# Three-column products and reordered outer products in the stencil stage of a convolution, attention and expert kernel

## The reference, cut to what matters

```python
offset = x1 @ off_w + off_b
mask = jax.nn.softmax((x1 @ mask_w + mask_b).reshape(N, H, W, G, P), -1)
...
samples = _bilinear_sample(img, sg)
out = (samples * m).sum(-1)
return out @ out_w + out_b
```

## Time and profile before

| what | value |
|---|---|
| median of three runs | 676.95 us |
| the profiled execution, its own time | 677.6 us |
| span of its trace | 675.7 us |
| busy: PE / DVE / ACT / POOL | 600.9 / 555.7 / 234.7 / 318.5 us |
| mean granted TensorE clock | 0.97 |
| products L1656 | 208 instructions, 216.8 us busy |
| outer products L1588, additions L1597 | 55.5 and 45.0 us busy |

### The profile page before, as it was taken

One profiled execution on the slowest core, in us unless ns is written; L12 is line 12 of the kernel. 1 busy time (PEld: TensorE's weight loads), 2 busy tenths in 40 slices (PEclk: granted clock), 3 DMA queues, 4 the chain that ended last, 5 costly groups with the idle time before them and its releaser, 6 DMA issues.

```text
span 675.7 us, 11172 instructions
## 1 busy us (share of the span) xinstructions
PE 600.9 (89%) x3668; PEld 448.7 (66%) x3668; DVE 555.7 (82%) x1028; ACT 234.7 (35%) x351; POOL 318.5 (47%) x408
## 2 busy tenths in 40 slices
PE   5989968979889889889696789999999999989995
PEld 4557556657567667666474677777777777785774
DVE  4677999999999999999999889847677766654877
ACT  6172504405207116135034000254544544415431
POOL 7504876787578588658578500202222211115222
PEclk9899989989999899899998899999999999989999
DMA  6196402103003007000000000000000000004111
GB/s 182 44 352 206 138 0 81 34 2 110 1 4 110 1 3 275 0 1 3 0 2 4 0 1 1 1 1 0 1 1 1 1 1 1 0 2 125 42 39 47
DMA packets 26244, 30.76 MB, mean 46 GB/s; under 512 B 5573, under 2 KB 18325, under 8 KB 26197
## 3 DMA queue, kind: packets, MB, share of 16 engines
q1 hardware_dynamic: 24094, 29.77, 13.4%
q0 software_dynamic: 1408, 0.36, 0.7%
q10 hardware_dynamic: 694, 0.01, 0.1%
HBM read 25.07 MB, written 5.05 MB: 45 GB/s over the span
## 4 chain that ended last, share of the span: by engine, by line
PE 44%; DVE 33%; issue 11%; ACT 2%; DVEq 0%; DMA 0%; SPq 0%; POOL 0%; ACTq 0%; POOLq 0%
DVE prod L1656 18%; PE banks L1061 9%; PE pair L1041 8%; PE banks L934 8%; DVE outer L1588 6%; PE pair L1129 4%; PE banks L1051 4%; PE banks L1167 4%; DVE hats L1539 1%; PE banks L921 1%; DVE stencil L1597 1%; PE banks L1012 1%; PE pair L864 1%; PE banks L956 1%; PE banks L1033 1%
## 5 line engine op out<-in xcount | busy, mean ns | idle before, releaser
L934 PE MATMUL banks<-ident,prod 128*128 128x128 f32 x1440 | 209.0, 288 | 44.6 <-DVE prod L1656 43.2
L934 PEld LDWEIGHTS banks<-ident,prod 128*128 128x128 f32 x1440 | 170.1, 147 | 99.4 <-DVE prod L1656 74.5
L1656 DVE TENSOR_TENSOR prod<-shifted,stencil 128x1024 f32<-128x1024 f32 (+1 forms) x208 | 216.8, 1084 | 7.6 <-ACT stencil L599 4.2
L1412 POOL TENSOR_TENSOR rstd_now<-mv_now,neg_half 128x2 f32<-128x2 f32 x32 | 23.0, 719 | 134.1 <-DVE mv_now L1704 134.1
L864 PE MATMUL pair<-xg,dw_diag 128*128 128x512 f32 x144 | 72.5, 604 | 1.4 <-DVE xg L1466 1.4
L1307 POOL DMA_INDIRECT got<-padded,cell_now x44 | 62.6, 1423 | 19.0 <-issue 10.1
L1061 PEld LDWEIGHTS banks<-shifted 128*128 128x128 f32 x512 | 60.2, 192 | 8.1 <-issue 6.1
L1061 PE MATMUL banks<-shifted 128*128 128x128 f32 x512 | 63.3, 277 | 2.3 <-ACT shifted L740 1.4
L1041 PE MATMUL pair<-shifted 128*128 128x512 f32 x128 | 60.6, 596 | 0.1
L1719 DVE TENSOR_REDUCE neg_max<-pair 128x1 f32<-128x1024 f32 x32 | 39.2, 1225 | 23.1 <-PE pair L1041 21.9
L1588 DVE TENSOR_TENSOR outer<-hats 128x800 f32<-128x800 f32 x56 | 55.5, 990 | 1.8 <-PE banks L921 1.8
(11 more groups left out here) (260 smaller groups left out, 956.4 us busy)
## 6 DMA issues: line engine op xcount, KB each, us to landing
shifted<-padded SPq DMA_DIRECT2D x42, 256.0 KB, 4.0
shifted<-padded SPq DMA_DIRECT2D x14, 640.0 KB, 8.1
res<-in_x_dram SPq DMA_DIRECT2D x4, 512.0 KB, 6.5
padded<-stage SPq DMA_DIRECT2D x4, 512.0 KB, 12.4
stage<-in_L_ffn_W_dram SPq DMA_DIRECT2D x16, 128.0 KB, 2.1
out_dram<-res SPq DMA_DIRECT2D x16, 128.0 KB, 1.8
got<-padded,cell_now POOLq DMA_INDIRECT x44, 3.0
padded<-stencil SPq DMA_DIRECT2D x2, 228.0 KB, 2.6
```

The source lines that it names most:

```text
L934: mm = pe.matmul(acc_of(c, r), prod[:, slot, r * G:(r + 1) * G, :].rearrange("p g c -> p (g c)"), ident[:, :], is_transpose=True, start=(t ...
L1656: ins = ve.tensor_tensor(prod[:, dx:dx + n, :, :], shifted[:, dx:dx + n, bass.ds(((c % HALF) * ROWS + dy) * G, ROWS * G), :], stencil_of[: ...
```

## The change

Units are now built a row at a time: the first unit of a row has three columns, the others two, so a row of seven is 3+2+2 and a row of five 3+2, 19 units in place of 26. `prod` keeps its seven slots. In a turn, an outer product signals its end itself and the vector engine goes on; in three of the nine steps (0, 2 and 5) a product now stands where it waited, and one unit follows each addition, two the last. PE's insertions move by a tap, the list of far points and the SiLU are taken earlier, chunk 0 gets fewer clock-keeping matmuls, and `copy_sums(0)` moves behind the copy of the offsets.

```diff
-UNIT_AT = [(t, 2 if t + 1 < NEAR and TAP_AT[t + 1] == (dy, dx + 1) else 1)
-           for t, (dy, dx) in enumerate(TAP_AT) if (dx - (dy in (0, WIN - 1))) % 2 == 0]
+def units_of(dxs):
+    return [3] + [2] * ((len(dxs) - 3) // 2)
+
+UNIT_AT = []
+for dy in ROW_ORDER:
+    taps = [t for t, at in enumerate(TAP_AT) if at[0] == dy]
+    for n in units_of(taps):
+        UNIT_AT.append((taps[0], n))
+        taps = taps[n:]
...
-AT_CONV, AT_FAR, AT_OFFSETS, AT_SAMPLES, AT_PROJECT = 4, 15, 30, 31, 35
+AT_CONV, AT_FAR, AT_OFFSETS, AT_SAMPLES, AT_PROJECT = 5, 16, 30, 31, 35
...
-FIRST_LIST, AT_LIST = 4, 3
+FIRST_LIST, AT_LIST = 4, 2
...
-AT_SILU = 5
+FIRST_SILU, AT_SILU = 5, 3
...
-POINT_FILL = (1, 2, 2, 2, 2, 2, 2, 2, 2)
+POINT_FILL = (1, 0, 1, 0, 0, 1, 0, 0, 0)
+STENCIL_FILL = (0, 1, 1, 1, 1, 1, 1, 1, 2)
...
-            copy_sums(0)
-            prepare(1)
+            prepare(1, sums_at=0)
...
-            for q in range(6):
+            for q in range(5):
                 sum_point(0, q)
-                keep_clock(4, bank[3])
+                keep_clock(2, bank[3])
             offsets(1, 0, ROWS)
-            for q in range(6, PTS):
+            for q in range(5, PTS):
                 sum_point(0, q)
-                keep_clock(3, bank[3])
+            keep_clock(6, bank[3])
...
-                    own(ve.tensor_tensor(to if q == 0 else outer[:, :, :, :],
...
-                    own.wait()
-                    ve.sem_inc(outer_done, 1)
-                    if q == PTS - 1:
-                        ve.sem_inc(hats_used, 1)
+                    ve.tensor_tensor(to if q == 0 else outer[:, :, :, :],
...
+                                     hx[:, :, q, :].unsqueeze(2).to_broadcast(full), ALU.mult).then_inc(outer_done, 1)
+                    fill(POINT_FILL[q])
                     if q > 0:
+                        ve.wait_ge(outer_done, PTS * k + q + 1)
+                        if q == PTS - 1:
+                            ve.sem_inc(hats_used, 1)
                         to = to[:, 0:DIRECT, :, :]
                         own(ve.tensor_tensor(to, to, outer[:, 0:DIRECT, :, :], ALU.add))
-                    fill(POINT_FILL[q])
+                    fill(STENCIL_FILL[q])
...
-                    ve.wait_ge(prod_free, c * NEAR + max(freed_by(t), freed_by(t + n - 1)) + PROD)
+                    ve.wait_ge(prod_free, c * NEAR + max(freed_by(t + i) for i in range(n)) + PROD)
```

More of the change, by code:

```diff
@@ L58 @@
 NEAR = len(TAP_AT)
-UNIT_AT = [(t, 2 if t + 1 < NEAR and TAP_AT[t + 1] == (dy, dx + 1) else 1)
-           for t, (dy, dx) in enumerate(TAP_AT) if (dx - (dy in (0, WIN - 1))) % 2 == 0]
+def units_of(dxs):
[6 more added lines that the diff above has]
+        taps = taps[n:]
 UNITS = len(UNIT_AT)
 BEGIN = 2
-AT_CONV, AT_FAR, AT_OFFSETS, AT_SAMPLES, AT_PROJECT = 4, 15, 30, 31, 35
-FIRST_LIST, AT_LIST = 4, 3
-AT_SILU = 5
-POINT_FILL = (1, 2, 2, 2, 2, 2, 2, 2, 2)
+AT_CONV, AT_FAR, AT_OFFSETS, AT_SAMPLES, AT_PROJECT = 5, 16, 30, 31, 35
[3 more added lines that the diff above has]
+STENCIL_FILL = (0, 1, 1, 1, 1, 1, 1, 1, 2)
 FIRST_POINT = BEGIN + 5
-POINT_UNIT = [FIRST_POINT + sum(POINT_FILL[:q]) for q in range(PTS)]
+POINT_UNIT = [FIRST_POINT + sum(POINT_FILL[:q]) + sum(STENCIL_FILL[:q]) for q in range(PTS)]
 SUMMED = 8
@@ L1587, in stencils @@
                         ve.wait_ge(outer_read, PTS * k + (q if q > 1 else 0))
-                    own(ve.tensor_tensor(to if q == 0 else outer[:, :, :, :],
-                                         hy[:, :, q, :].unsqueeze(3).to_broadcast(full),
-                                         hx[:, :, q, :].unsqueeze(2).to_broadcast(full), ALU.mult))
-                    own.wait()
-                    ve.sem_inc(outer_done, 1)
-                    if q == PTS - 1:
-                        ve.sem_inc(hats_used, 1)
+                    ve.tensor_tensor(to if q == 0 else outer[:, :, :, :],
+                                     hy[:, :, q, :].unsqueeze(3).to_broadcast(full),
+                                     hx[:, :, q, :].unsqueeze(2).to_broadcast(full), ALU.mult).then_inc(outer_done, 1)
+                    fill(POINT_FILL[q])
                     if q > 0:
+                        ve.wait_ge(outer_done, PTS * k + q + 1)
+                        if q == PTS - 1:
+                            ve.sem_inc(hats_used, 1)
                         to = to[:, 0:DIRECT, :, :]
                         own(ve.tensor_tensor(to, to, outer[:, 0:DIRECT, :, :], ALU.add))
-                    fill(POINT_FILL[q])
+                    fill(STENCIL_FILL[q])
                 own.wait()
@@ L1630, in first_stencils @@
                         list_far(0)
-                    if q == AT_SILU:
+                    if q == FIRST_SILU:
                         finish_silu(1)
```

## The result

The changed kernel took 688.89, 693.37, 684.56 and 684.75 us, a median of 686.82, where the kernel before took 676.92 beside it: a ratio of 1.0164 on record, 95% interval 1.0113 to 1.0214 (the two medians divide to 1.0146). I had said 680.0 and a range of 674 to 686: the direction was right, the size was not.

What follows compares the result with a forecast made beforehand. The prediction took DVE (VectorE) to bound the stencil stage. Costs of 21.65 less gains of 18.5 gave +3.1 us on the profiled 677.6, so 680.7; less 0.65 to the median, 680.0 us, range 674 to 686 (8 of 10).

Steps and rivals of the forecast that it cites:

- Units and pauses: Stencil stage on DVE: 7 fewer units in each of 8 chunks save 4.5 us, shorter outer-to-addition pauses 9.0 us.
- Start and waits that go: Chunk 0's first unit starts 3.0 us earlier; DVE's waits in turn 0 and before the last chunk shrink, saving 2.0 us.
- First, the products between the convolution matmuls: Turns 0 to 5: DVE's products wait 1.6 us a turn for slots until PE's taps are read, costing 9.6 us.
- Second, `copy_sums`: ACT's three hats stand ahead of `copy_sums`, so a chunk's first unit waits 1.1 us more in six turns: 6.6 us.
- Third, `outer_read` at outer 7: Turns 1 to 5: DVE waits 0.85 us before outer 7 for `sum_point` 6 in PE's queue, costing 4.25 us.
- Fourth, the clock: PE's thinner work between steps 1 and 5 makes half-clock stretches likelier; 0.2 us in six turns, 1.2 us, bounds 0 and 6.
- the clock's rival: Half clock reaches the work before `sum_point` 6, third wait grows up to 1.6 us in six turns: 685 to 690; chance 0.15.
- The list of far points, at nothing: Moving the list and the SiLU up in DVE's queue costs nothing, as 7 us of DVE work covers PE's count.

## Why the prediction was wrong

- **Units and pauses, 4.5 and 9.0 us: right.** A product of 1536 elements took 1.763 us in the mean, one of 1024 1.224; the outer-to-addition gap fell by 0.10. Without far points the pauses alone take a turn from 47.6 to 46.36; I had 1.29 a turn.
- **Start and waits that go, 3.0 and 2.0: right** at 2.6 and 2.1 (0.82, and 1.62 to 0.34 before the last chunk).
- **First, the products between the convolution matmuls, 9.6: right in size** at 9.9 (five waits of 1.59, 1.47, and 0.46 once). The runs add that this isn't the price of one slot: moved or split, the wait comes back elsewhere. Work with two-column units passes the same stretch in a turn of 46.4 us. That the grain is what matters, since a product of three columns waits for three slots and hands over three taps at once, is argued and not shown: the places of the list, the SiLU and TensorE's insertions differ too, and no run has more slots.
- **Second, `copy_sums`, 6.6: about right in size, half wrong in cause.** The waits before a first unit sum to 8.5, 0.6 of which stood there before. They were 1.12 to 1.17 in four turns and 1.89 and 1.98 in turns 1 and 3, where TensorE was at a granted clock of 0.83 (150 to 160 us) and 0.73 (255 to 261); there its taps and not ScalarE's queue decide. Some 1.6 of the 7.9 added are the clock's, then.
- **Third, `outer_read` at outer 7, 4.25: 6.4** without GpSimd and with TensorE kept busy; 1.20 a turn in place of 0.85, and 0.40 in turn 0, which I had left out.
- **Fourth, the clock, 1.2: 4.6. This is the first step that failed: a term of the sum with the right mechanism and a quarter of its size.** I had allowed 0.2 us a turn and had kept 6 as a bound and the rival. The mechanism was the one I named, short bursts of taps with idle time between them, then half clock. I priced it low because the kernel before showed one swing with a price, though it had no such thin stretch to show. At half clock three taps took 2.61 us after as before; what I had wrong is how often that makes VectorE wait before outer 5, in five turns of six and not in fewer than half, and for how long, 0.54 to 0.80 us and not 0.45. By the rule in the Trainium skill, "TensorE: Matmul & The Clock Gate", section "A second HAM failure mode: psum-queue depth-cycling", which I had weighed and set below the trace, the clock's rival was the likeliest; the traces agree with the rule as far as the stretches at 0.50 and the 4.6 us of waits behind them.
- **The list of far points, at nothing: 3.7. This is the second step that failed.** I priced moving the list by when TensorE counts the points; that held, since VectorE never waits before the list. But I left GpSimd out. The move put the `MAX8` in front of a row whose pause is filled, where it held GpSimd 4.9 to 7.5 us a turn, and the other filled pauses slowed GpSimd too. What had covered it was a lead of some 8 us in turn 4 and the pauses that the change removes.

Together: costs of 9.9 + 7.9 + 14.7 - 1.75 (the last turn's wait of before, gone) = 30.8 in place of 21.65, gains 18.2 in place of 18.5: +12.6, where VectorE's stage ended 11.9 us later (439.93 against 428.05) and the span grew by 11.3. So the sum closes in the trace of one execution; the median grew by 9.9.

## What to carry to other kernels

Filling an engine's pauses can take them from another engine: before a pause is closed, find the engine that needs it, what stands in front of the pause, and how far ahead of its reader that engine is. A wait that is taken from one engine goes to the next one with no slack, so two edits that each gain can lose together; measure them one at a time and then in pairs. And where an edit leaves TensorE with short bursts, price the stretch at half clock, not at the clock that the kernel before shows.

## What the runs showed that I had not expected

- A GpSimd instruction of 0.73 us in the mean before took up to 5.63 us, and another of 1.5 us up to 7.5, where VectorE ran a `MAX8` and then 5.8 us more without a gap; a gap of 0.03 to 0.04 us was enough for six of the seven to end. In rows without a gap that had no `MAX8` GpSimd's instructions ended one after the other.
- Twelve to sixteen small matmuls a turn that nobody reads took away the half-clock stretches they were put into and gained nothing in either kernel, through a third engine (a ratio of 1.0261 where the change alone had 1.0164; 0.9948 in place of 0.9893, with intervals that overlap). Only without the far points did they pay: 1.0039 in place of 1.016.
- The mean granted clock of one kernel, the changed one without far points, differed between executions (0.951 to 0.963), and 5 us of its time with it.
